# Edge quads of a graph layer: ten gathered from x itself, counts from two one-hots, layernorm and tail rewritten

## What is computed

```python
h = jnp.maximum(_layernorm(x, axis=-1), 0.0)
e = jnp.concatenate([hid[src_idx], hid[dst_idx]], axis=1)
m = jax.nn.relu(e @ W1 + b1) @ W2 + b2
s = jax.ops.segment_sum(m, dst_idx, num_segments=n_nodes)
cnt = jax.ops.segment_sum(jnp.ones((m.shape[0],), dtype=m.dtype), dst_idx, num_segments=n_nodes)
return s / jnp.maximum(cnt, 1.0)[:, None]
x = x + _L0_gnn_ref(h, L0_gnn_W1, L0_gnn_b1, L0_gnn_W2, L0_gnn_b2, src, dst)
```

## Time and profile before

| | us |
|---|---|
| median of 3 runs | 2181.44 (2179.91 to 2184.9) |
| profiled execution | 2186.75 |
| its span | 2184.9 |

### The profile page before, as it was taken

The page is one execution under the profiler, slowest core; times in us unless marked ns, Lnnn a source line. Parts: engine busy times, 40 slices in busy tenths (PEclk is TensorE's granted clock), DMA queues, the critical chain, the costliest instruction groups (busy, mean ns, idle before and its releaser), DMA issues.

```text
span 2184.9 us, 28891 instructions
## 1 busy us (share of the span) xinstructions
PE 1491.1 (68%) x9104; PEld 1303.1 (60%) x9105; DVE 992.4 (45%) x2112; ACT 295.3 (14%) x503; POOL 1543.3 (71%) x1610
## 2 busy tenths in 40 slices
PE   5786666666666666666666666666666666666799
PEld 5676555555555555555556555565555555555687
DVE  6664444444444444444444444444444444444200
ACT  4311111111111111111111111111111111111100
POOL 5677777777777777777777777777777777777300
...
DMA packets 112904, 151.25 MB, mean 69 GB/s; under 512 B 32653, under 2 KB 83212, under 8 KB 112750
## 3 DMA queue, kind: packets, MB, share of 16 engines
...
...
q10 hardware_dynamic: 564, 0.23, 0.1%
...
## 4 chain that ended last, share of the span: by engine, by line
POOL 62%; issue 21%; PE 9%; DMA 4%; DVE 2%; DVEq 0%; ACT 0%; SPq 0%; POOLq 0%
POOL g L375 62%; DMA g<-p_table,src_e 3%; PE bank L855 3%; PE bank L856 3%; PE bank L799 2%; PE bank L727 1%; PE bank L796 1%; DMA xs<-in_x_dram 1%; DVE g L609 0%; DVE acc L617 0%; DVE area L511 0%; DVE area L620 0%; PE bank L720 0%; DVEq L612 0%; ACT area L434 0%
## 5 line engine op out<-in xcount | busy, mean ns | idle before, releaser
L375 POOL DMA_INDIRECT g<-p_table,src_e x1563 | 1503.6, 962 | 493.9 <-issue 421.1
L609 DVE TENSOR_TENSOR g<-bank,g 128x512 f32<-128x512 f32 x391 | 270.4, 691 | 1034.1 <-DMA g<-p_table,src_e 1008.5
L796 PE MATMUL bank<-member,ones 128*1 128x128 bf16 x1563 | 167.0, 233 | 651.9 <-DVE area L620 651.4
L799 PE MATMUL bank<-member,g 128*128 128x128 f32 x3126 | 582.4, 343 | 0.0
L790 PEld LDWEIGHTS bank<-qw,spread 128*128 128x128 f32 x3126 | 542.6, 245 | 43.1 <-DVE spread L593 8.2
L790 PE MATMUL bank<-qw,spread 128*128 128x128 f32 x3126 | 527.7, 325 | 7.4 <-DVE spread L593 7.4
L796 PEld LDWEIGHTS bank<-member,ones 128*1 128x1 bf16 x1563 | 95.7, 85 | 723.2 <-DVE member L599 714.9
L799 PEld LDWEIGHTS bank<-member,g 128*128 128x128 f32 x3126 | 489.8, 239 | 54.8 <-issue 18.1
L466 ACT ACTIVATE g<-g 128x512 f32<-128x512 f32 x391 | 246.1, 629 | 1714.9 <-DVE g L609 1714.9
L593 DVE TENSOR_SCALAR spread<-bank,rows_f 128x512 f32<-128x512 f32 x391 | 286.3, 732 | 9.9 <-DMA area<-spread 8.7
L599 DVE TENSOR_TENSOR member<-columns,rel_e 128x512 f32<-128x512 f32 x391 | 266.9, 683 | 0.0
...
## 6 DMA issues: line engine op xcount, KB each, us to landing
qw<-q_table SPq DMA_DIRECT2D x391, 64.0 KB
g<-p_table,src_e POOLq DMA_INDIRECT x1563, 2.6
...
```

What stands on the lines that cost most here:

```text
L375: nc.gpsimd.indirect_dma_start(out=g[0:ROWS, k, j * HID:(j + 1) * HID], out_offset=None, in_=p_table, in_offset=bass.IndirectOffsetOnAxis( ...
L609: nc.vector.tensor_tensor(rows_n, z_bank[n % 2][0:ROWS, 0:w], rows_n, ALU.add).then_inc(z_done, 1)
L796: nc.tensor.matmul(to[0:1, WIN:2 * WIN], ones16[0:ROWS, :], ones_and_zeros(k, c), start=c == 0, stop=c == chunks - 1)
L799: last = nc.tensor.matmul(to[:, 0:WIN], rows_n[:, HID * c:HID * (c + 1)], member[0:ROWS, k, c, :], start=c == 0, stop=c == chunks - 1)
```

## The change

- **Ten raw quads.** `RAW = 10`: for quads 0 to 9 GpSimd gathers rows of x (40 gathers of 128 x 64) as soon as a small index load `idx_raw` has landed. VectorE takes their statistics, ScalarE normalises them (`raw_h`), TensorE turns them (`raw_t`), and in the quad loop each chunk's product gets two matmuls more: `ones_row` times `b1_row`, and `raw_t` times W1. `add_rows` falls away for these quads. P gathers begin with quad 10; `RING` is 18.
- **Layernorm without GpSimd.** `bn_stats` for each tile and five small instructions for each load on VectorE, scale, shift and relu in one ScalarE instruction for each tile. P is now copied by VectorE with b1, Q by ScalarE without. Nodes lie in pairs on the partitions (`x_v`, `out_v`, `p_v`, `q_v`), so DRAM pieces are 512 or 1024 bytes, not 5120.
- **src tables.** Table 0 is made in the P part, tables 1 to 3 behind the root of the raw rows' statistics.
- **W2 per quad.** ScalarE copies the hidden sums (`sums_u`), one matmul with W2 gives 64 rows, VectorE adds them to `sums`.
- **Counts.** The ones products and the count add fall away. Each dst is split into two digits (28 small steps from quad 14 on), and from quad 44 to 335 VectorE makes two one-hots of 100 and 125 columns for each quad (1.34 pairs an iteration); their product is added up in one PSUM bank. b2 is added to x in the loop after that.
- **Columns in PSUM.** The member matrix and the one-hots read the column numbers from `columns_p` in PSUM.
- **Tail.** 100 transposes of `sums`, in 13 batches of eight tiles; VectorE scales, VectorE and GpSimd add.

```diff
-RING = 16
+RAW = 10
+RING = 18
+HOTS = 3
+DIGITS_FROM, COUNT_FROM, COUNT_TO, SCALE_FROM = 14, 44, 335, 338
+BT = 8
...
+        columns_p = bank[7][:, 0:WIN]
...
-            for n in range(GROUPS):
-                centre(n)
-                square(n)
+            pool.wait_ge(idx_in, 16)
+            for n in range(RAW):
+                for j in range(4 * n, 4 * n + 4):
+                    nc.gpsimd.indirect_dma_start(
+                        out=raw_h[:, j, :], out_offset=None, in_=x,
+                        in_offset=bass.IndirectOffsetOnAxis(ap=idx_raw[:, j:j + 1], axis=0)).then_inc(raw_in[n], 16)
...
             pool.wait_ge(src_table, QT)
...
-                if n >= RING:
+                k = slot(n)
+                if k == 7 and turn(n) == 0:
+                    for m in range(STAGES):
+                        pool.wait_ge(q_out[m], q_all_out[m])
+                if n >= RAW + RING:
                     pool.wait_ge(u_psum, n - RING + 1)
...
+                for i in range(GT):
+                    t = n * GT + i
+                    last = nc.scalar.activation(hs[n % HS][:, i, :], xs[:, t, :], ACT.Relu,
+                                                bias=shift_n[0:NP, t:t + 1], scale=rstd[0:NP, t:t + 1])
...
-            nc.scalar.copy(acc[:, :], zeros[:, 0:1].to_broadcast([128, ACOLS])).then_inc(v_zero, 1)
+            nc.scalar.copy(sums[:, NE:2 * NE], zeros[0:FEAT, 0:1].to_broadcast([FEAT, NE])).then_inc(v_zero, 1)
...
+                for t in range(n * XT, (n + 1) * XT):
+                    last = nc.vector.bn_stats(stats[:, t, :], xs[:, t, :])
...
-                                        columns[0:ROWS, :].unsqueeze(1).to_broadcast([ROWS, 4, WIN]),
+                                        columns_p.unsqueeze(1).to_broadcast([128, 4, WIN]),
...
-                nc.vector.tensor_tensor(c, c, u_bank[n % 2][0:1, WIN:2 * WIN], ALU.add).then_inc(c_done, 1)
+                nc.vector.tensor_tensor(v, v, u_bank[n % 2][0:FEAT, WIN:2 * WIN], ALU.add).then_inc(v_done, 1)
...
+                    if n < RAW:
+
+                        nc.tensor.matmul(z, ones_row[:, :], b1_row[:, :], start=True, stop=False)
+                        nc.tensor.matmul(z, raw_t[:, n, c // 2, :], w1[:, c % 2, 0, :], start=False, stop=False)
...
+                nc.tensor.matmul(u_bank[n % 2][0:FEAT, WIN:2 * WIN], w2[:, :], sums_u[:, n % 2, :],
+                                 start=True, stop=True).then_inc(v_psum, 1)
...
-                    nc.tensor.matmul(to, acc[:, node], w2[:, :], start=True, stop=False)
-                    last = nc.tensor.matmul(to, count[:, node], b2_row[:, :], start=False, stop=True)
+                    last = nc.tensor.transpose(bank[b % 8][0:NP, FEAT * (t % BT):FEAT * (t % BT + 1)],
+                                               sums[:, first:first + 2 * NP - 1:2], ident[0:FEAT, 0:FEAT])
```

843 lines of the change are left out of this document (510 added, 333 removed).

## The result

| | median of the runs (us) | lowest to highest | profiled execution, its span |
|---|---|---|---|
| before | 2180.7 | 2177.0 to 2184.9 | 2186.75, 2184.9 |
| changed | 3078.8 | 3068.2 to 3114.3 | 3114.33, 3112.5 |

The ratio is 1.410, with a 95% interval from 1.403 to 1.418. I had forecast 2020 us, within 1996 to 2055; slower than before had a chance of 0.03.

The account below looks back on a forecast made before the run. GpSimd issuing gathers was taken to bound the kernel; -50.7 (forty gathers fewer), -28 (cheaper gathers), +6.5 (start), +16 (stop) and -105 (tail) made -161 on 2184.9, a 2023.5 us span, forecast 2020 us, range 1996 to 2055.

Parts of the forecast that it names:

- slower than before: Rival: TensorE becomes the bound between quads 44 and 335, 5.6 us a quad at half clock, 2197 us; chance 0.03.
- The counts ride in the loop: Quad loop with counts: VectorE 3.6 and TensorE 3.7 to 4.2 us a quad, below GpSimd's 4.99, so no cost.
- if that cover is gone: Counted quads: should GpSimd's pace no longer hide the work, each 0.1 us over 4.99 costs 29 us over 291 quads.
- first table gather: Start of GpSimd's P-table gathers: at 71 us (67 to 76), against 64.45 before.
- a step: Time from one GpSimd gather to the next: 1.248 us instead of 1.2665, over 1522 steps, -28 us.
- stop at quad 28: GpSimd waits there until quad 11 is summed: 16 us, bounds 4 and, all cold, 67.
- Gathers and contention: Quad loop: reading columns from PSUM leaves VectorE one SBUF input, so gathers take 0.94 us, not 1.42; -28 us.
- The start: Before the quad loop: the first table gather waits for ScalarE's src tables, behind the raw statistics; +6.5 us.
- The raw quads: First ten quads: 5.6 us each, bounds 4.0 and 10.7 at half clock; clock rising 6 us after start at 114.
- Rival (b): Raw quads: the clock stays at half through them, stop 67 us, 2071 us in all; chance 0.08.
- The tail: After the last gather: 37 us against 142.2, with 100 transposes in 21.5 us at half clock; -105 us.
- the marks that I had named as showing the prediction wrong: Mean gather near 962 ns; VectorE not awaiting gathers, quads 44 to 335; quad 28 gap over 40 us; TensorE tail gaps.

Follow-up runs that it names:

- e3_lag2: The changed kernel with VectorE's add of the sums moved one round earlier (quad n-2 in round n); 2052.3 us, 0.941 of before.
- e8: The changed kernel, late add kept, with the counts' one-hots placed behind the sums' add in VectorE's round; repeated run 2352.0 us, 1.081 of before.
- e1: The kernel before with only VectorE's add of the sums moved one round later; 2593.9 us, 1.190 of before.
- e5: e3_lag2 with the column numbers for member matrix and one-hots read from SBUF, not PSUM; repeated run 2127.9 us, 0.973 of before.
- e4: The changed kernel, late add kept, without the counts' one-hots and count products; 2124.6 us, 0.976 of before.
- e6: e3_lag2 with b1 of the ten raw quads added by VectorE, not by a one-row product; repeated run 2025.5 us, 0.928 of before.
- e9_b1_src_c: e6 with the last three src tables made before ScalarE's square root of the raw rows' statistics; third run 2025.5 us, 0.928 of before.

## Why the prediction was wrong

**The step that failed** is "The counts ride in the loop ... Both stay below GpSimd; cost nothing." I compared each engine's busy time a quad (VectorE 3.6, TensorE 3.7 to 4.2) with the pace of 4.99. Those sums were nearly right: e3_lag2 shows 3.58 for VectorE and 3.58 for TensorE. But "stays below" presumes that the engines work beside each other, and whether they do is decided by the waits. The change moves an add by one round, and the prediction does not mention it: I had followed GpSimd's and ScalarE's queues past every wait, but not VectorE's add. What the runs showed in its place: in the counted quads the spread product, rows' add, member matrix, one-hots, sums' add, sums, W2 and count products follow one another in a ring of 7.9 us a quad on average, and moving the add back gives 849 us in that stretch and 1026 in all. Slower had a chance of 0.03, for a TensorE whose own work at half clock (5.6 us) is the bound. That mechanism is not what happened, but the clock has a share in what did: of the 2.9 us over the pace some 1.1 are the ring's length at full clock and 1.8 its rounds at a lower one (an estimate, from e8's rounds above). The sentence "if that cover is gone, each 0.1 us a quad over 4.99 costs 29 us" was right too: 2.9 us over make 850, and 849 were measured.

To be seen in advance it would have taken one more look at the earlier trace rows: 3.35 + 2.34 = 5.7 us a quad if TensorE and VectorE were to take turns, already over 4.99 (measured in e1: 4.44 at full clock, 6.6 at half), and then a walk from the wait of the sums (on the add of n-2) to where that add now stands.

**The other terms**, read off e3_lag2, where the ring is open (span 2049.2, my sum 2023.5):

| term | predicted | in e3_lag2 |
|---|---|---|
| first table gather | 71 (67 to 76) | 78.0 |
| a step | 1.248 | 1.251 |
| stop at quad 17, for the Q stores | not seen | 1.8 |
| stop at quad 28 | 16 | 24.0 |
| behind the last gather | 37 | 41.1 |

- **Gathers and contention: right.** 1523 gathers, 944 ns, and 946 against 998 between e3 and e5, which differ only in where the column numbers are read. The Trainium skill (SBUF — State Buffer, "Who interferes with whom") says that a VectorE instruction with at most one SBUF input does not contend with GpSimd, and that one with two contends with a GpSimd instruction that reads SBUF. The traces agree.
- **The start: the mechanism right, the size off.** It is released by ScalarE's src table, as said. The opening of the changed kernel:

```profile
68.70 5.16 DVE L601 BATCH_NORM_STATS2 raw_stats<-raw_h 128x6 f32<-128x64 f32 x40
...
75.07 2.01 ACT L434 CAST src_e<-bank 128x512 int32<-128x512 f32 x2
...
79.20 0.94 POOL L370 DMA_INDIRECT g<-p_table,src_e  x1 [25.29 <-ACT src_e L434]
```

 A statistic cost 5.16 / 40 = 0.13 us, the low bound. The small steps, for whose 0.2 us no row of before was named, took 0.19 to 0.23 us each, the reciprocal 0.40. But the 64-column activations of h cost 0.34 us each and not 0.21 (L422, 100 in 34.3 us), ten groups 13 us more; VectorE begins the raw statistics at 68.70, right behind its last P add, where I had 59.6.
- **The raw quads: right at full clock, the clock wrong.** 5.80 us a quad at full clock (predicted 5.6) and 10.4 at half (10.7). I let the clock rise 6 us after the start, as in the kernel before; it took 18 us in e3 and 101 in the changed kernel's trace. Rival (b), all cold, had 67 us of stop: the changed kernel's trace has 64.8, but that is one execution's clock, since the same raw quads stop GpSimd for 24 to 28 us in five other traces, with the late add (e4, e8_b) and without it. The first quad came at 124, not 114: ScalarE's Q groups at 2.8 and not 2.6 us each, from a later start, and 4 us of waiting for Q stores beside the zeros. Of the price of a one-row product and its changes the runs show only the sum: e6 took 0.61 us off a chunk at full clock and 1.02 at half.
- **The tail: right.** In e3_lag2:

```profile
2019.55 21.26 PE L1030 MATMUL bank<-ident,acc 64*125 64x64 f32 x100 [4.59 <-issue]
```

 100 transposes in 21.26 us (21.5 predicted), at half clock. The 4 us more: 11.5 from the last gather (2008.09) to the first transpose instead of 8.7, 3.8 of them "issue" behind the last add, and 8.4 behind the last transpose instead of 6.7.

Of the marks that I had named as showing the prediction wrong, two did: VectorE no longer waits for gathers between quads 44 and 335 (its L727 waits 209.5 us for TensorE's L950 and for no gather), and the gap at quad 28 was over 40 us. The first is the ring. The second came true by luck, by the clock of the profiled execution.

The best kernels of these are e6_b1_vector_b and e9_b1_src_c, 2025.5 us; e6 is the change with its add moved back by a round and b1 of the raw quads on VectorE, 7.2% faster than before. That it lies within my range says little for the forecast: it is another kernel, and its gain on the raw quads makes up for a start that I had 7 us too early.
